# The fp4 scaling of a fused attention and feed-forward kernel: one small product folded into the large one behind it

## The reference

```python
def fp4_quant_dequant(x):                      # blocks of 16 along the last dim
    xb = x.reshape(shape[:-1] + (shape[-1] // BLOCK, BLOCK))
    scale = jnp.max(jnp.abs(xb), axis=-1, keepdims=True) / 6.0
    scale = jnp.maximum(scale, jnp.float32(1e-12))
    xn = xb / scale
    idx = jnp.searchsorted(_MID, jnp.abs(xn))
    return (_GRID[idx] * jnp.sign(xn) * scale).reshape(shape)

gate, y = fp4_linear(x, w_gate), fp4_linear(x, w_up)
h = jax.nn.silu(gate) * y
out = fp4_linear(h, w_down)
```

## Time and profile before

| what | value |
|---|---|
| median of three runs | 3527.69 us |
| the profiled execution, its own time | 3532.97 us |
| its span in the trace | 3531.2 us |
| granted TensorE clock, mean | 0.988 of full speed |
| TensorE busy | 3420.3 us, 97% |
| VectorE busy | 2947.5 us, 83% |
| ScalarE busy | 2298.8 us, 65% |
| GpSimd busy | 1036.9 us, 29% |

### The profile page before, as it was taken

One profiled execution on the slowest core, in us unless ns is written; L12 is line 12 of the kernel. 1 busy time (PEld: TensorE's weight loads), 2 busy tenths in 40 slices (PEclk: granted clock), 3 DMA queues, 4 the chain that ended last, 5 costly groups with the idle time before them and its releaser, 6 DMA issues.

```text
span 3531.2 us, 55990 instructions
## 1 busy us (share of the span) xinstructions
PE 3420.3 (97%) x19606; PEld 1560.4 (44%) x19606; DVE 2947.5 (83%) x6697; ACT 2298.8 (65%) x4512; POOL 1036.9 (29%) x1114
## 2 busy tenths in 40 slices
PE   7899999999999999999999999999999999999996
PEld 3333444444444444444444444444444444444334
DVE  6878888888888988888888888988888888888865
ACT  2667666667666667666667666667666667666662
POOL 1323222333322333222333322333222333322222
PEclk7999999999999999999999999999999999999998
DMA  4332233232232332233232232332232232232210
GB/s 81 57 51 45 39 57 50 34 62 36 49 51 44 53 44 45 40 57 48 36 62 35 49 52 43 54 44 43 42 57 46 38 62 32 49 55 35 38 24 8
DMA packets 154263, 163.02 MB, mean 46 GB/s; under 512 B 58071, under 2 KB 127080, under 8 KB 153984
## 3 DMA queue, kind: packets, MB, share of 16 engines
q1 hardware_dynamic: 153984, 159.45, 28.6%
HBM read 46.22 MB, written 8.39 MB: 15 GB/s over the span
## 4 chain that ended last, share of the span: by engine, by line
PE 72%; DVE 23%; ACT 2%; POOL 1%; issue 1%; DMA 1%; SPq 1%; ACTq 0%; DVEq 0%
PE out_ps L912 18%; PE score_ps L901 16%; PE piece_ps L926 16%; DVE piece_max L1264 13%; PE work L865 6%; PE work L876 4%; PE work L840 3%; PE work L832 3%; ACT probs L1028 1%; PE work L856 1%; PE work L821 1%; DVE ctx_T L1134 1%; DVE ctx_T L1130 1%; PE work L850 1%; PE work L873 1%
## 5 line engine op out<-in xcount | busy, mean ns | idle before, releaser
L1028 ACT ACTIVATE probs<-score_ps 128x512 f32<-128x512 f32 (+1 forms) x3328 | 1884.0, 600 | 923.7 <-PE score_ps L901 916.0
L1264 DVE TENSOR_REDUCE piece_max<-piece_ps 128x1 f32<-128x400 f32 (+1 forms) x4096 | 2110.3, 566 | 360.6 <-PE piece_ps L926 347.8
L926 PE MATMUL piece_ps<-k_stack,q_stack 96*128 96x400 bf16 (+1 forms) x4096 | 1297.5, 339 | 40.2 <-DVE piece_max L1264 28.2
L901 PE MATMUL score_ps<-q_stack,k_stack 99*128 99x512 bf16 (+1 forms) x3328 | 1252.2, 385 | 19.6 <-DMA q_stack<-neg_rows 5.3
L912 PE MATMUL out_ps<-probs,v_ones 128*17 128x512 f32 x6656 | 877.1, 599 | 0.4
L926 PEld LDWEIGHTS piece_ps<-k_stack,q_stack 96*128 96x128 bf16 x4096 | 386.0, 98 | 801.9 <-DVE piece_max L1264 548.2
L901 PEld LDWEIGHTS score_ps<-q_stack,k_stack 99*128 99x128 bf16 (+1 forms) x3328 | 324.2, 99 | 641.7 <-ACT probs L1028 494.4
L1316 POOL TENSOR_TENSOR h<-h,h_grid 128x704 f32<-128x704 f32 (+1 forms) x68 | 111.8, 1644 | 888.4 <-DVE h_grid L1092 888.4
L865 PE MATMUL work<-wgu_T,xq_T 128*128 128x512 f32 (+1 forms) x1080 | 333.7, 425 | 0.5
L912 PEld LDWEIGHTS out_ps<-probs,v_ones 128*17 128x17 f32 x6656 | 110.3, 95 | 269.4 <-issue 218.4
L865 PEld LDWEIGHTS work<-wgu_T,xq_T 128*128 128x128 f32 x1080 | 198.1, 191 | 43.9 <-issue 3.8
(11 more groups left out here) (173 smaller groups left out, 2893.4 us busy)
## 6 DMA issues: line engine op xcount, KB each, us to landing
k_stack<-k_parts SPq DMA_DIRECT2D x256, 150.1 KB, 3.6
k_stack<-k_parts SPq DMA_DIRECT2D x256, 100.1 KB, 3.9
ctx_in<-in_ctx SPq DMA_DIRECT2D x47, 384.0 KB, 3.8
k_stack<-k_parts SPq DMA_DIRECT2D x256, 50.0 KB, 3.7
q_stack<-q_parts SPq DMA_DIRECT2D x256, 48.0 KB, 2.8
x_in<-in_x SPq DMA_DIRECT2D x16, 512.0 KB, 5.0
q_stack<-q_parts SPq DMA_DIRECT2D x256, 32.0 KB, 2.1
resid<-in_x SPq DMA_DIRECT2D x62, 128.0 KB, 2.6
```

The costliest lines, as they stand in the source:

```text
L901: pe.matmul(score_ps[0:r, n % SCORE_RING, :], k_stack[:, par, slot(g, j), m * P:m * P + r], q_stack[:, par, slot(g, j), :], start=True, st ...
L926: pe.matmul(piece_ps[:, n % PIECE_RING, 0:hi - lo], q_stack[0:SROWS, par, slot(g, j), t * P:(t + 1) * P], k_stack[0:SROWS, par, slot(g, j) ...
L1028: act.activation(probs[0:r, step % 2, j, :], score_ps[0:r, (PER_GROUP * m + j) % SCORE_RING, :], ACT.Exp, scale=SCORE_SCALE).then_inc(prob ...
L1264: dve.tensor_reduce(piece_max[:, row, c:c + 1], piece_ps[:, n % PIECE_RING, 0:piece_at[c + 1] - piece_at[c]], AX_X, ALU.max).then_inc(piec ...
```

## The change

`fp4_small` loses its third instruction. The factor `BELOW_TIE` goes into the large product as its scalar: `fp4_scale` is now one `scalar_tensor_tensor` that computes (rows x `BELOW_TIE`) x reciprocal, in place of a `tensor_tensor` that computes rows x (reciprocal x `BELOW_TIE`). The chain has six steps a tile (`ROUNDING`) and the counts of the semaphores follow. Nothing else is touched: the order of all other instructions on all engines is the same.

```diff
+ROUNDING = 6
...
             def fp4_small(small, done, base):
 
-                amax, scale, inv = (small[:, i, :] for i in range(3))
+                amax, scale = small[:, 0, :], small[:, 1, :]
                 dve.wait_ge(done, base(1))
                 dve.tensor_scalar(scale, amax, 1.0 / 6.0, TINY, ALU.mult, ALU.max).then_inc(done, 1)
                 dve.wait_ge(done, base(2))
                 dve.reciprocal(amax, scale).then_inc(done, 1)
+
+            def fp4_scale(src, small, done, base):
                 dve.wait_ge(done, base(3))
-                dve.tensor_scalar(inv, amax, BELOW_TIE, None, ALU.mult).then_inc(done, 1)
-
-            def fp4_scale(src, small, done, base):
-                dve.wait_ge(done, base(4))
                 n = src.shape[1] // BLOCK
-                dve.tensor_tensor(fp4_blocks(src), fp4_blocks(src), over_block(small[:, 2, :], n), ALU.mult).then_inc(done, 1)
+                dve.scalar_tensor_tensor(out=fp4_blocks(src), in0=fp4_blocks(src), scalar=BELOW_TIE, in1=over_block(small[:, 0, :], n),
+                                         op0=ALU.mult, op1=ALU.mult).then_inc(done, 1)
...
             def fp4_grid(src, grid, done, base):
 
+                dve.wait_ge(done, base(4))
+                dve.tensor_scalar(grid.bitcast(I32), src.bitcast(I32), EXPONENT_BITS, None, ALU.bitwise_and).then_inc(done, 1)
                 dve.wait_ge(done, base(5))
-                dve.tensor_scalar(grid.bitcast(I32), src.bitcast(I32), EXPONENT_BITS, None, ALU.bitwise_and).then_inc(done, 1)
-                dve.wait_ge(done, base(6))
                 dve.tensor_scalar(grid, grid, 1.0, ROUNDER, ALU.max, ALU.mult).then_inc(done, 1)
```

More of the change, by code:

```diff
@@ L1206, in handle @@
                     fp4_max(q.xq, q.xq_small, xq_step)
-                    fp4_small(q.xq_small, xq_step, lambda k: count(old, 7 * QT, 7 * t + k))
+                    fp4_small(q.xq_small, xq_step, lambda k: count(old, ROUNDING * QT, ROUNDING * t + k))
                 elif name == "xq_scale":
-                    base = (lambda k: count(old, 7 * QT, 7 * event[1] + k))
+                    base = (lambda k: count(old, ROUNDING * QT, ROUNDING * event[1] + k))
                     if kind != "tail" and (old or event[1]):
@@ L1225, in handle @@
                     t = event[1]
-                    base = (lambda k: count(old, 7 * QT, 7 * t + k))
+                    base = (lambda k: count(old, ROUNDING * QT, ROUNDING * t + k))
                     src = q.h
@@ L1237, in handle @@
                         if kind == "tail" and t in VECTOR_ROUNDS:
-                            fp4_round(src, q.h_grid, q.h_small[:, 1, :], h_step, base(7), *rounds_of(kind, old, t))
+                            fp4_round(src, q.h_grid, q.h_small[:, 1, :], h_step, base(ROUNDING), *rounds_of(kind, old, t))
                 elif name in ("w_max", "w_scale", "w_grid"):
                     i = event[1]
-                    base = (lambda k: 7 * i + k)
+                    base = (lambda k: ROUNDING * i + k)
                     src = w_view(i)
@@ L1359, in handle @@
                     t = event[1]
-                    fp4_round(q.xq, q.xq_grid, q.xq_small[:, 1, :], xq_step, count(old, 7 * QT, 7 * (t + 1)),
+                    fp4_round(q.xq, q.xq_grid, q.xq_small[:, 1, :], xq_step, count(old, ROUNDING * QT, ROUNDING * (t + 1)),
                               xq_round, lambda k: count(old, 3 * QT, 3 * t + k))
@@ L1365, in handle @@
                         return
-                    fp4_round(q.h, q.h_grid, q.h_small[:, 1, :], h_step, count(old, 7 * QT, 7 * (t + 1)),
+                    fp4_round(q.h, q.h_grid, q.h_small[:, 1, :], h_step, count(old, ROUNDING * QT, ROUNDING * (t + 1)),
                               h_round, lambda k: rounds_of(kind, old, t)[1] + k)
@@ L1371, in handle @@
                     r, w = src.shape
-                    fp4_round(src, h_grid[0:r, 0:w], h_small[0:r, 1, 0:w // BLOCK], w_step, 7 * (i + 1),
+                    fp4_round(src, h_grid[0:r, 0:w], h_small[0:r, 1, 0:w // BLOCK], w_step, ROUNDING * (i + 1),
                               w_round, lambda k: 3 * i + k)
```

## The result

| | before | after |
|---|---|---|
| median of four runs each, same chip | 3527.99 us | 3505.47 us |
| lowest to highest | 3524.78 to 3530.14 | 3502.89 to 3506.86 |
| the profiled execution, its own time | 3532.97 us | 3506.86 us |
| its span | 3531.2 us | 3505.1 us |
| granted TensorE clock, mean | 0.988 | 0.991 |

The ratio is 0.9934 [0.9922, 0.9946]: 22.5 us or 0.64% faster. The forecast was 3509 us, in a range of 3499 to 3525, from a sum of 18.9 us. The length of a body is the time from one start of L1183 to the fourth behind it. It is given as a median because in each trace four to six of the 13 bodies are over 0.1 us longer than it, by up to 2.8 us; the means, 212.21 and 211.00 us, give the same difference as the medians.

A forecast was written before the change was run, and what follows sets the result against it. TensorE and VectorE were taken to bound the kernel in turns, in stretches of a few us. The terms 7.5 + 3.1 + 3.3 + 2.4 + 1.3 + 1.3 = 18.9 us off the 3527.69 us median gave 3509 us, range 3499 to 3525.

The forecast's parts named there:

- (b): The xq step of each body's second quarter: TensorE idles after it and takes up 0.21 us, 15 times, 3.1 us.
- Rival 4: Slower: the new product takes a second pass, 0.74 us more on h and 0.27 on xq; 3541 us, chance 0.05.
- (a): The xq step of each body's first quarter, where L1071 waits for GpSimd: TensorE takes up 0.50 us, 15 times, 7.5 us.
- the three covered steps: The xq steps of the third and fourth quarter and the h step of the fourth: hidden behind TensorE, worth nothing.
- The other four steps: Four steps in each body after which TensorE is behind and sets the pace: removing L1071 there counts for nothing.
- rival 2: More than the chain: TensorE's late stretches hang on VectorE too, or old GpSimd meetings vanish; below 3503 us, chance 0.10.
- (c): The h step of each body's second quarter: TensorE idles 0.34 us and takes up 0.22, 15 times, 3.3 us.
- (d): The h step of the third quarter, off the chain: TensorE's piece could begin 0.17 us earlier, 14 times, 2.4 us.
- (e): The first body: seven removed instructions on the chain, one gaining nothing; 6 x 0.22 = 1.3 us.
- (f): The tail, one chain without cover: 6 x 0.21 = 1.3 us.

The follow-up runs named there:

- e_plain: Changed kernel with its large product as a plain tensor_tensor, BELOW_TIE left out: 3506.90 us, ratio 0.9944 to the kernel before.
- e_keep: Kernel before with the new scalar_tensor_tensor product, L1071 still issued but its result unused: 3527.59 us, ratio 1.0000.
- e_xq0: Kernel before with the fold only at the xq step of each body's first quarter: 3519.95 us, ratio 0.9979.
- e_covered: Kernel before with the fold only at the xq steps of the third and fourth quarter and the h step of the fourth: 3527.93 us, ratio 1.0000.
- e_two_h: Kernel before with the fold only at the h steps of each body's second and third quarter: 3521.30 us, ratio 0.9982.
- e_four: Kernel before with the fold only at the xq step of the first quarter and the h steps of the first three: 3510.48 us, ratio 0.9951.
- e_ends: Kernel before with the fold only in the first body's weights' rounding and the whole tail: 3522.55 us, ratio 0.9987.
- e_noport: Kernel before with L1071 of the first quarter's xq step replaced by a second reciprocal, factor left out there: 3519.69 us, ratio 0.9979.

## Why the prediction was right

The time, the sign and the main term were right; the sum of 18.9 was 3.6 us short of the 22.5 measured, from errors of both signs. That they nearly cancel is luck: (b) put 3.1 us too much into the sum, while the `h` step of the first quarter and what all eight steps give beyond their single sums, 0.13 + 0.23 = 0.36 us a body or 5.4 in all, were not in it.

- **The product costs nothing**: right (887 and 886 ns; e_plain, e_keep). Rival 4, the second pass, is out.
- **(a), 15 x 0.50**: right. 0.49 in e_xq0, and 0.50 between the piece and its score matmul. That the product would lose something to L1351 unfelt was right too: 0.15 us, put at 0.25.
- **(b), 15 x 0.21**: this step failed. It said that "all of VectorE's stretch from there to 1207.5 is on the chain". Inside that stretch the chain has 0.07 us of waiting, for a piece that TensorE delivers only then. It was worth 0.01 us alone, and 0.14 a body together with the three covered steps when the other four are folded too.
- **The other four steps, nothing**: three of them yes (e_covered), the `h` step of the first quarter no. The rule used, that TensorE isn't waiting within the next us, asks about TensorE alone. The step's product goes on to GpSimd, whose last instruction meets the norm step on VectorE's path some 8 us later: 0.13 to 0.18 us a body. The line had a maximum of 959 ns in the kernel before, and the prediction did not look for it; it is rival 2's "old meetings with GpSimd vanish".
- **(c) and (d), 0.22 and 0.17**: right, 0.25 and 0.16 in e_two_h.
- **The bodies in sum**: 1.10 us forecast, 1.22 measured, so 18.3 us of the whole by 15 bodies. "A body of 210.9" came out as 210.73, above the 210.4 that rival 2 set.
- **(e) and (f), 2.6 us**: not settled. 22.5 - 18.3 = 4.2 are left for the ends. e_four gained 17.1, which is 5.4 less than the changed kernel; with 15 x 0.14 = 2.1 of these in the bodies, 3.3 are left. e_ends gave 5.0. All three are above 2.6, but the interval of e_ends, 1.4 to 7.4, holds it. The sum had no term for the clock of the last matmuls, 2.83 to 5.46 us. At the earlier trace rows the product now takes 0.67 us in place of 1.50, and the next instruction, L1090, 1.20: the wait moved and gave nothing, as the sum had it.
- **TensorE's waits** fell by 24.8 us, against 15 to 20, and VectorE's busy time by 34.7 against 36 to 37: the rows of L1071 in the kernel before add up to 35.6 us, L1202 gained 3.3, and the 15 products at (a) gave 2.3 back; about 2 us of the sum of these are not accounted for.

The prediction's price for a removed instruction, 0.19 us for the tile, came from rows. The page of the Trainium skill that it set beside this (VectorE: DVE Perf Modes, the errata section) also gives, beside the 58 cycles that I quoted, about 150 cycles as the fixed part that was measured. That would be some 0.16 us, an estimate from the page, without the part that grows with the columns; the traces' 174 and 186 ns are near it.

What stays open: why the norm step gains a further 0.06 us (0.81 to 0.75) and the second interval 0.12 when the steps are folded all together, and how often the tail's matmuls get the fast clock.

## What to carry to other kernels

Before a small instruction is priced, list the min, median and max of its line, and do the same for all lines of that engine that the change does not touch: a maximum of more than twice the median at a fixed place in each round was here, both times, a meeting with GpSimd, and it changed when something ahead of either engine moved. Between two engines in turns, follow the chain from the edit to the next wait of either engine, however short: at a wait of 0.07 us most of a gain of 0.2 us ended here. Where a meeting is on the path, reorder the instruction out of it; one number in a table gave 0.27 us a body here, a fifth of the 1.22 that the removal of the small products gave.

## What the runs showed of the hardware

In these kernels VectorE's `tensor_scalar` and its products of two SBUF tiles do not end before a GpSimd `tensor_tensor` that already runs: L1071 took 911 ns in place of 174 beside a GpSimd instruction of 1.15 us, the norm step up to 959 in place of 404 beside one of 1.39, and the 128x256 product 582 in place of 416 beside one of 0.72. Reciprocals and maxima in the same places were not held up: the second reciprocal of e_noport, beside the same GpSimd product, took 252 to 254 ns in all 15 bodies, and the maximum at 1149.73, which reads PSUM, started while L1347 ran. The Trainium skill (SBUF — State Buffer, "Who interferes with whom") has this as a lock for the whole instruction, taken by whichever of the two starts first, that spares VectorE instructions with one SBUF input outside the 2-port modes, and names `tensor_scalar` among those that can enter such a mode. The traces agree for the reciprocal (252 to 254 ns) and the products (582); in which mode L1071 and the norm step ran they do not show.

A `scalar_tensor_tensor` with both inputs in SBUF costs no more than the `tensor_tensor` of its shape, 887 against 886 ns at 128x704 in fp32. The same 12 matmuls at the end took 5.46, 4.2 to 4.4 or 2.83 us, with 0.50, 0.64 to 0.67 or 1.00 of the clock granted over them; between two kernels with the same tail that made 1.6 us (2.83 and 4.41).
